# Adjacency mixing, a 128-step recurrence and a top-2 mixture of experts: expert rows handled in halves of 64, both passes written out, two early stages reordered

## The reference

```python
beta = einsum('bld,du->blu', layernorm(x), e_weight) / maximum(sum(graph, 2), EPS)[:, :, None]
agg = einsum('blu,blm->bmu', beta, graph)
h = tanh(agg[:, t] @ Wx + h @ Wh + b)            # for t = 0..127, kept as ys
x = x + ys
g = layernorm(x)
topk_vals, topk_idx = top_k(g @ gate_w + gate_b, 2)          # 16 experts, per token
h = relu(g @ w1[e] + b1[e]); o = h @ w2[e] + b2[e]           # for the two experts e
y = g + sum(softmax(topk_vals) * o)
out = x + (y - mean(y)) / sqrt(var(y) + EPS) * gamma + beta_
```

## Time and profile before

| | |
|---|---|
| median of 3 runs | 685.48 us (685.31 to 685.70) |
| profiled execution | 684.95 us, its span 683.2 us |
| busy in the span | PE 533.3 us, DVE 512.2, POOL 465.5, ACT 414.1 |
| mean granted TensorE clock | 0.913 |

### The profile page before, as it was taken

One profiled execution on the slowest core, in us unless ns is written; L12 is line 12 of the kernel. 1 busy time (PEld: TensorE's weight loads), 2 busy tenths in 40 slices (PEclk: granted clock), 3 DMA queues, 4 the chain that ended last, 5 costly groups with the idle time before them and its releaser, 6 DMA issues. The chain is left out here.

```text
span 683.2 us, 17528 instructions
## 1 busy us (share of the span) xinstructions
PE 533.3 (78%) x4152; PEld 477.9 (70%) x4152; DVE 512.2 (75%) x2551; ACT 414.1 (61%) x1350; POOL 465.5 (68%) x526
## 2 busy tenths in 40 slices
PE   1767699799989720999999999702999999999950
PEld 1656477577777610799999999700799999889840
DVE  5989489799989760688888888600488898889970
ACT  2889656466656301566666666400789899889940
POOL 3667707677777775277777777775277777777774
PEclk9999999999999755899999999955999999999985
DMA  8999749533433131689876655441997666664110
GB/s 215 279 268 287 199 126 303 162 106 115 120 101 101 56 121 41 164 274 313 253 222 209 195 188 172 151 153 55 338 339 226 201 211 201 210 187 143 47 52 7
DMA packets 115099, 121.44 MB, mean 178 GB/s; under 512 B 19017, under 2 KB 99613, under 8 KB 115008
## 3 DMA queue, kind: packets, MB, share of 16 engines
q1 hardware_dynamic: 94784, 75.71, 39.4%
q0 software_dynamic: 17920, 43.03, 17.4%
q10 hardware_dynamic: 2304, 1.64, 0.8%
HBM read 68.67 MB, written 55.90 MB: 182 GB/s over the span
## 5 line engine op out<-in xcount | busy, mean ns | idle before, releaser
L224 POOL DMA_INDIRECT rows_by_second<-R x144 | 145.3, 1009 | 60.2 <-issue 36.6
L224 POOL DMA_INDIRECT out_dram<-R x144 | 142.5, 990 | 61.1 <-issue 38.7
L1064 PE MATMUL bank<-W,hs 128*128 x1152 | 175.7, 288 | 0.0
L1126 ACT ACTIVATE hs<-bank,wr 128x128 f32<-128x128 f32 x432 | 127.4, 367 | 70.3 <-PE bank L1048 63.9
L224 POOL DMA_INDIRECT rows_by_first<-st x128 | 125.7, 982 | 59.3 <-issue 35.3
L1048 PE MATMUL bank<-xT,wr 128*128 128x128 f32 x1152 | 155.7, 278 | 8.7 <-ACT xT L1107 8.7
L1064 PEld LDWEIGHTS bank<-W,hs 128*128 128x128 f32 x1152 | 151.3, 191 | 3.4
L1048 PEld LDWEIGHTS bank<-xT,wr 128*128 128x128 f32 x1152 | 139.8, 192 | 15.9 <-ACT xT L1107 15.8
L1199 DVE SCALAR_TENSOR_TENSOR R<-bank,R 128x128 f32<-128x128 f32 x288 | 87.0, 344 | 58.4 <-PE bank L1064 57.8
L1115 ACT COPY wr<-W1b 128x258 f32 x288 | 104.4, 422 | 0.2
L548 ACT ACTIVATE HT<-bank,bcol 128x128 f32<-128x128 f32 x128 | 47.0, 367 | 58.9 <-PE bank L454 55.9
(11 more groups left out here) (138 smaller groups left out, 867.9 us busy)
## 6 DMA issues: line engine op xcount, KB each, us to landing
R<-rows_by_second SPq DMA_DIRECT2D x140, 196.0 KB
R<-rows_by_first SPq DMA_DIRECT2D x140, 68.0 KB
xq<-in_x_dram SPq DMA_DIRECT2D x32, 256.0 KB, 4.1
aq<-in_adj_dram SPq DMA_DIRECT2D x32, 256.0 KB, 5.0
x2r<-in_x_dram SPq DMA_DIRECT2D x32, 256.0 KB, 2.8
rows_by_second<-filler SPq DMA_DIRECT2D x1, 3136.0 KB, 12.3
rows_by_second<-filler SPq DMA_DIRECT2D x16, 196.0 KB
rows_by_second<-R POOLq DMA_INDIRECT x144
```

What stands on the lines that cost most here:

```text
L224: return nc.gpsimd.indirect_dma_start(dst, bass.IndirectOffsetOnAxis(ap=idx, axis=0), src, None, bounds_check=limit[n], oob_is_err=False)
L1064: i = mm(o, hs[:, h, c, k * P:(k + 1) * P], W2[:, bass.ds(e[k], 1), c, :].rearrange("p o f -> p (o f)"), start=False, stop=c == 1, skip_gr ...
L1126: i = a(hs[:, h, c, k * P:(k + 1) * P], ps_h[c][h][:, k * P:(k + 1) * P], ACT.Relu, bias=wr[:, u % 2, 2 * h + k, F + c:F + c + 1])
```

## The change

Blocks are counted in halves of 64. An expert with h halves of rows gets floor(h / 2) whole blocks, and a half that is left over shares a block with another expert's: 128 whole blocks and 8 mixed ones, so 32 plain and 2 mixed quads, 34 in a pass. In a mixed quad each block is loaded with two DMAs of 64 rows, `wr` holds two experts' weights for each block, the first product is done in columns of 64, the relu writes into `hm` (whose other half stays zero), and the second product adds both experts' terms into the same 128 rows. The scatters stay one for each block. The loops of the passes go, every quad is written out.

```diff
-    NBLK = P + NE
-    NQUAD = NBLK // QUAD
+    HALF = P // 2
+    NPURE = P // QUAD
+    NQUAD = NPURE + NE // 2 // QUAD
 # both passes
+        def mixed(q):
+            return q >= NPURE
+        def parts(G):
+            return ((0, 0, HALF), (1, HALF, HALF)) if mixed(G % NQUAD) else ((0, 0, P),)
 # first() on PE
-                            i = mm(ps_h[c][h][:, (j % 2) * P:(j % 2 + 1) * P], wr[:, u % 2, j, c * P:(c + 1) * P],
-                                   xT[:, u % 2, j * P:(j + 1) * P], start=True, stop=True)
+                            for s, lo, n in parts(G):
+                                at = j % 2 * P + lo
+                                i = mm(ps_h[c][h][:, at:at + n], wr[:, u % 2, s, j, c * P:(c + 1) * P],
+                                       xT[:, u % 2, j * P + lo:j * P + lo + n], start=True, stop=True)
 # POOL, ahead of pass 1
+                pool.wait_ge(tables, 1)
+                g.memset(hm[:, :, :, :, :], 0.0)
+                g.memset(sel_half[:, :, :, :], 0.0).then_inc(e_mix, 1)
+                pool.wait_ge(e_mix, 1)
+                for s in range(2):
+                    half = sel_half[:, s, :, HALF * s:HALF * s + HALF]
+                    g.tensor_copy(half, sel[:, :, HALF * s:HALF * s + HALF]).then_inc(e_mix, 1)
```

In the aggregation POOL makes its constants and `sel` ahead of the first scale, and `single(q)` scales the first two and the last two quads one by one. In the recurrence, the first quad's input term is split so that the first tanh needs 128 of its 512 columns, and the orders change:

```diff
 # steps() on PE
-                    if k == 0 and not (isinstance(q, int) and q == NQ - 1):
-                        fresh(q + 1, u + 1)
-                    if k == 1 and beyond(q, 1):
-                        turn_h(q - 1, u - 1)
-                    if k == 1 and beyond(q, 2):
-                        logits(q - 2, u - 2)
-                    if k == 2 and beyond(q, 4):
-                        count(q - 4, u - 4)
+                    if k == 0 and q > 0:
+                        turn_h(q - 1, u - 1)
+                    if k == 0 and q > 3:
+                        count(q - 4, u - 4)
+                    if k == 1 and q > 1:
+                        logits(q - 2, u - 2)
+                    if k == 2 and q < NQ - 1:
+                        fresh(q + 1, u + 1)
 # even(t) on DVE, before:
-  tile_a, tile_b, gate_4, tile_b2, gate_5, tile_b3, place_1, root_0, soft_2, sq_0, place_2, ag_0, soft_3, in_0, place_3, ou_0, ..., ou_1
+  tile_a, place_1, soft_2, place_2, soft_3, place_3, tile_b, gate_4, tile_b2, gate_5, tile_b3, root_0, sq_0, ..., ou_1
 # odd(t) on DVE:
-  tile_a, tile_b, gate_1, tile_b2, gate_2, place_1, gate_3, place_2, apart, gate_4, place_3, gate_5
+  tile_a, place_1, gate_1, place_2, gate_2, place_3, gate_3, apart, gate_4, gate_5, tile_b, tile_b2
 # SP: between the loads of x2r, in place of all after the 8th
+                if q in (11, 15):
+                    h = (q - 11) // 4
+                    rows = TAIL + h * NE // 2 * P
+                    filled(dram_b.ap()[rows:rows + NE // 2 * P, :], W_B, NE // 2).then_inc(s_fill, 16)
+                if q in (19, 23):
+                    h = (q - 19) // 4 * NE // 2
+                    sp.dma_start(W1b[:, h:h + NE // 2, 0:F],
+                                 w1[h:h + NE // 2].rearrange("e h f -> h e f")).then_inc(r_w, 16)
+                if q == 27:
...
```

More of the change, by code:

```diff
@@ L375, in _ @@
             rest()
+            for q in (0, 1):
+                single(q)
+            for u in range(2, SLOTS):
+                scale(u, u)
+            with pool.Fori(1, NQ // SLOTS - 1) as J:
+                for u in range(SLOTS):
+                    scale(SLOTS * J + u, u)
+            for q in range(NQ - SLOTS, NQ - 2):
+                scale(q, q % SLOTS)
+            for q in (NQ - 2, NQ - 1):
+                single(q)
             for q in range(NQ):
@@ L474, in _ @@
             turn_h(NQ - 1, UN - 1)
+            count(NQ - 4, UN - 4)
             logits(NQ - 2, UN - 2)
-            count(NQ - 4, UN - 4)
             turn_x(NQ - 1, SLOTS - 1)
+            count(NQ - 3, UN - 3)
             logits(NQ - 1, UN - 1)
-            for n in range(3, 0, -1):
+            for n in range(2, 0, -1):
                 count(NQ - n, UN - n)
@@ L831, in even @@
                 one(tile_a, t - 1)
+                one(place_1, t - 4)
+                pair(soft_2, p - 1)
+                one(place_2, t - 4)
+                pair(soft_3, p - 1)
+                one(place_3, t - 4)
                 one(tile_b, t - 1)
@@ L836, in even @@
                 pair(tile_b3, p)
-                one(place_1, t - 4)
                 pair(root_0, p)
-                pair(soft_2, p - 1)
                 pair(sq_0, p)
-                one(place_2, t - 4)
                 pair(ag_0, p)
-                pair(soft_3, p - 1)
                 pair(in_0, p)
-                one(place_3, t - 4)
                 pair(ou_0, p)
@@ L1077, in quad @@
                     first(G, u, 0)
-                    e = experts(r, q)
-                    if not start:
-                        second(r, G - 1, 1, e[0:2])
+                    at = first_of(q)
+                    m = 2 * QUAD if mixed(q) else QUAD
+                    e = experts(r, at)
+                    if m > QUAD:
+                        e = e + experts(r, at + QUAD)
+                    if q > 0:
+                        second(r, G - 1, 1, held[r] + e[0:2])
                     first(G, u, 1)
@@ L1121, in relu @@
                     act.wait_ge(e_h, n + 1)
-                    if not (isinstance(G, int) and G < 1):
+                    if G >= 1:
                         act.wait_ge(e_o, n - 1)
@@ L1142, in quad @@
                     if start:
-                        for j, e in enumerate(experts(r, q)):
+                        e = experts(r, q)
+                        for j in range(QUAD):
                             weights(r, q, G, u, j, e)
```

319 lines of the change are left out of this document (190 added, 129 removed).

## The result

The changed kernel takes 663.01 us at the median of four runs (659.54 to 663.37), the kernel before 685.39 in the same comparison: ratio 0.9664, 95% interval 0.9635 to 0.9693, so 22.4 us or 3.4% faster. The profiled execution is the quickest of the four: 659.54, span 657.8, mean granted clock 0.926. In a second comparison the same kernel had 661.62 (660.45 to 662.77) against 685.11, ratio 0.9658 [0.9639, 0.9678]. The forecast was 660.6, the range 656 to 667.

What follows compares the result with a forecast made beforehand. Both passes were taken as bound by POOL's number of indirect DMAs (scatters). Terms -0.8 - 2.2 - 2.0 - 10.5 + 1.0 - 10.4 = -24.9 us took the profiled 684.95 to 660.05, median forecast 660.6; range 656 to 667.

Steps and rivals of the forecast that it cites:

- The passes: Both passes: 8 scatters fewer in each at unchanged price, 10.5 us less in pass 1 and 10.4 in pass 2.
- Rival 5: Passes: the number of scatters is not their pace (64-row loads or the ring are), so 681.5 us; chance 0.03.
- The x2r stall: Stage two: moving the `b1` loads off SP's queue removes DVE's 4.66 us wait for `x2r`, 2.0 us less.
- The first scatter: Start of stage two: `place_1` and `place_3` come earlier, so the first scatter is 2.2 us earlier, bounds 1 to 4.
- `turn_h` one step earlier adds nothing: Ahead of stage two's first scatter: PE's reordering is worth 0, as DVE's list sets the pace.
- (c): Stage two: `place` and `soft` lose the square root's shade, 0.7 us per pair of quads; POOL stays fed, 0 to 3.5 us.
- Aggregation: First stage: constants first +1.0, last quads scaled singly -1.2, shorter product before the first tanh -0.6; together -0.8 us.
- DVE's list: Stage two: DVE's routing takes 4.96 us a quad, 10.49 / 2 at the bound, against POOL's 5.14.
- rival 4: Stage two: `count` waiting for `hot` puts DVE and PE steps in series, 704 us at 6.5 a quad; chance 0.03.
- Between the stages: Gap into pass 1: POOL's new memsets and copies may hold DVE's `zed`, +1.0 us, bounds 0 and 3.6.
- Rival 1: End of pass 2: PE and ACT become the limit, cover only 1.4 us; 1 to 4 us more, about 663; chance 0.15.
- The cover of the tables: End of stage two: tables and `b2` list grow 6 us but stay hidden behind POOL's scatters, about 3 us cover left.

Runs made afterwards that it cites:

- the passes alone: Changed passes, tables and written-out loops; aggregation, stage two and SP's loads as in the kernel before: 665.53 us against 685.16, ratio 0.9717.
- the constants late: Changed kernel with POOL's constants and `sel` back behind the last scale, single scales kept: 659.55 us, ratio 0.9617 to the kernel before.
- old list: Changed kernel with DVE's routing list in the old interleaved order, PE's and ACT's orders as changed: 863.48 and 854.15 us, both on the third chip.
- masks in the gap: Changed kernel with zeroing and copies for `hm` and `sel_half` on DVE, idle ahead of pass 1: 901.11 us on the third chip, 657.42 (ratio 0.9585) elsewhere.
- masks and constants: Changed kernel with `hm` and `sel_half` set up on DVE ahead of pass 1, POOL's constants behind the last scale: 904.5 and 885.79 us, third chip.

## Why the prediction was right, and where it was off

The sum of -24.9 met -25.4 in the profiled execution, and the time was 2.4 us above the forecast at the median of the first runs, 1.0 in the second comparison. That the sum fits so closely is in part luck: the execution is the quickest of its four, with the earliest first tanh of nine and the shortest gap into pass 1 of five; the medians differ by 22.4 and 23.5 us. The large terms hold one by one, and with them the mechanism; some of the small ones were wrong, in both directions.

**The passes** (-10.5 and -10.4): measured -10.0 and -10.4, and shown by the passes alone. Scatters cost what they cost before, 177.96 / 135 = 1.318 and 175.68 / 135 = 1.301 us, mixed quads and written-out code included. Rival 5 is out.

**The x2r stall** (-2.0): -1.9, and 3.7 when it is put back.

**The first scatter.** The step "`turn_h` one step earlier adds nothing, as DVE's list sets the pace there" failed: PE sets the pace of the first quads, and the earlier trace rows had the sign of it, a `tile_a` that waits 0.40 us for PE. The order is worth 1.4 us. The other half was over-sized: `place` ahead of the rest brings 1.5 us and not 2.2, because the price of DVE's longer list, counted in (c) against POOL's pace alone, also falls ahead of the first scatter (0.9 us). Together -2.9, inside the bounds of -1 to -4, since the two errors lie on opposite sides.

**Aggregation** (-0.8 = +1.0 - 1.2 - 0.6): the tanh's own wait fell by 0.64, as forecast. The mean of the nine executions is 77.4 against 78.06, so -0.6 in all. How the other two terms share the rest is open: with the constants at 1.7 in the mean, the single scales bring 1.7 by difference; by the executions of the one chip that has both, the constants cost 0.2 and the single scales bring 0.6 (78.18 in the passes alone, 76.96 with the constants late). No run took the single scales out alone, and the nine executions, whose aggregation is the same, differ by up to 1.9 us at this point.

**DVE's list** (4.96 us a quad taken, 10.49 / 2 at the bound): 5.05 measured, POOL 5.15. POOL was fed, as forecast, but with only 0.1 us to spare. PE's `count` waits for `hot` 19.5 us in 21 places over the stage, the wait of rival 4, but the period stayed far under its 5.92.

**Between the stages** is the step that failed most: "+1.0, since most of the memsets are over before the first rows land", with bounds of 0 and 3.6. Measured +2.8 to +4.3, at its worst beyond the bound. The copies, and not the memsets, were the ones that `zed` met, and half of the loss was not in the sum at all: a wait at this place costs the clock of the matmuls behind it, too. The price of holding DVE was bounded; what DVE's delay does to PE was not asked. The Trainium skill (SBUF — State Buffer, Who interferes with whom) has the holder of the shared port keep it for its whole instruction, where DVE works in a two-port mode. `zed` lost 1.4 us beside two copies of together 2.02 us, which fits with that; the 3.6 us of the long memset were never at stake, since it ended 0.04 us before `zed` began. The scatter that took 2.86 us beside DVE's memset was held for a whole instruction too, though the section names copies, casts and `tensor_scalar` as the operations that take the port, and not memsets.

**Rival 1,** the end of pass 2 turned to PE and ACT, did not come, and its cover was mis-sized: 4.0 us, not 1.4. POOL needs the last pair 174.4 us behind the first scatter of pass 2, as forecast; DVE has it ready at 170.4 and not 173.0. Of these 2.6 us about 1.4 are the mixed quads: 16 products of 64 columns take 1.90 us where 8 of 128 take 1.06, and with its transposes and second products a mixed quad adds up to about 8.5 us on PE (1.84 + 1.73 + 4.45 + 0.45 from start to start), not 9.2. Where the rest comes from was not tried.

**The cover of the tables** was mis-sized the other way, 0.5 us and not 3: POOL ended its stage 6.3 us earlier where 5 were taken, and the last operation of the `b2` list ended 7.6 us later than the tables before where 6 were taken. More than one or two further operations of this kind there would reach past POOL's last scatter.

**The end** gave 1.3 us that no step names: from last scatter to end of span 5.8 in place of 7.1. It comes with the passes (5.9 in the passes alone). Its cause was not tried.

## What to carry to other kernels

Where one engine's queue of equal DMAs paces a stage, count them and look for the first and last; everything else is judged by whether it reaches that queue. Ask of each wait what it does to the matmuls behind it: a turn that came 1.4 us late cost another 1.4 in clock here, and the same was seen once in the next gap and once in the middle of stage two. It is part of what differs between executions: the two profiled ones of the changed kernel lie 2.1 us apart, 1.1 of it in the gap into pass 1 and 0.9 ahead of the first scatter. Set-up work belongs into time in which both DVE and POOL idle, not merely the engine that does it: 4.2 us less came from moving four operations from POOL to DVE and a few us ahead.

## What was not expected of the hardware

A scatter's issue on POOL was held by a DVE memset for about its full length (2.86 us in place of 0.97 beside one of 1.76, twice).

Behind PE's waits of 1.74 to 2.86 us ahead of pass 1 (five executions), of 1.25 us ahead of pass 2 (one) and of 3.13 us in stage two (one) its granted clock was 0.50 to 0.59 for the next products, near the level of 1.2 GHz; behind waits of 0.29 to 0.73 us ahead of pass 1 it was 0.98 to 1.00 (three). Ahead of the passes warming matmuls ran in all of these and did not prevent it. Not every wait of that length costs the clock: in stage two of the changed kernel `count` waits up to 2.7 us for `hot`, and the granted clock of each stretch of 20 us from 110 to 230 us is still 0.91 to 1.00.

On one chip all kernels took 854 to 910 us, the kernel before 881 and 864, and the order of the kernels was another: as ratios to the kernel before, old list 0.988 and 0.985, masks in the gap 1.02, masks and constants 1.036 and 1.026, and the changed kernel by the medians 1.03 (one of its six executions took 862.86 us, the others 906 to 914). So a gain of this change is not shown for a chip in this condition. Instructions of ACT and POOL took their usual time (ACT is busy for 405.7 us against 407.2, a scatter of stage two takes 974 ns), PE was busy for 624.0 us against 530.7 at a mean granted clock of 0.835 against 0.926. The aggregation ran as elsewhere, but from the second stage on engines stood still again and again. ACT in the changed kernel there:

```profile
148.59 0.37 ACT L593 ACTIVATE HT<-bank,bcol 128x128 f32<-128x128 f32 x1 [6.75 <-remote]
...
164.85 0.37 ACT L593 ACTIVATE HT<-bank,bcol 128x128 f32<-128x128 f32 x1 [6.79 <-remote]
```

"Remote" names no instruction of this core. PE's product for the tanh at 148.59 had ended at 142.3. There are 13 such waits of the tanh for 32 quads, at most 7.5 us long and 77.5 us in all; the 128 scatters take 261.6 us there, and 218.7 and 217.0 with DVE's old list, whose first execution has 13 as well, but shorter ones (at most 4.9 us, 42.1 in all). What stops the engines there, and why the old order bears it better, stays open; it was not tried.
